# First attention of a fused transformer kernel: values of two steps on end in every second step, probabilities in eight buffers

## The reference

```python
# 32 query heads, 8 key/value heads, head size 16, after the rotation of q and k
scores = jnp.einsum('bhqd,bhkd->bhqk', q, k) / math.sqrt(HEAD_DIM)
scores = jnp.where(causal[None, None, :, :], scores, jnp.float32(-1e+20))
attn = jax.nn.softmax(scores, axis=-1)
out = jnp.einsum('bhqk,bhkd->bhqd', attn, v)
```

## Time and profile before

| | |
|---|---|
| median of the runs | 1273.1 us |
| the profiled execution, its own time | 1276.3 us |
| its span, from the first to the last instruction | 1274.6 us |
| busy: TensorE, weight loads, VectorE | 1179.1, 743.4, 928.0 us |
| busy: ScalarE, GpSimd | 655.5, 375.6 us |
| mean granted clock of TensorE | 0.94 |

### The profile page before, as it was taken

The page is one execution under the profiler, slowest core; times in us unless marked ns, Lnnn a source line. Parts: engine busy times, 40 slices in busy tenths (PEclk is TensorE's granted clock), DMA queues, the critical chain, the costliest instruction groups (busy, mean ns, idle before and its releaser), DMA issues.

```text
span 1274.6 us, 21543 instructions
## 1 busy us (share of the span) xinstructions
PE 1179.1 (93%) x6800; PEld 743.4 (58%) x6800; DVE 928.0 (73%) x2974; ACT 655.5 (51%) x1007; POOL 375.6 (29%) x505
## 2 busy tenths in 40 slices
PE   4998999999889998999989899999997999989888
PEld 1875343444358997545878644444432889855478
DVE  5789878999527878662768799899991578676365
ACT  1721556666555644444546026666666465445542
POOL 1431232222145520214624314111223455002261
PEclk9997679999899999899999958999999999989999
DMA  9465411121001013200250752112200100430001
GB/s 315 145 165 108 134 26 27 27 73 56 2 1 52 2 34 92 68 2 1 71 180 24 200 133 77 27 27 60 69 3 1 52 2 1 100 93 2 1 10 58
DMA packets 40309, 80.39 MB, mean 63 GB/s; under 512 B 6060, under 2 KB 7596, under 8 KB 40060
## 3 DMA queue, kind: packets, MB, share of 16 engines
q1 hardware_dynamic: 40200, 79.02, 21.8%
HBM read 48.98 MB, written 27.08 MB: 60 GB/s over the span
## 4 chain that ended last, share of the span: by engine, by line
PE 72%; DVE 14%; issue 5%; ACT 3%; DMA 3%; POOL 2%; SPq 1%; DVEq 0%; ACTq 0%; POOLq 0%
PE bank L1029 16%; PE bank L897 12%; PE bank L804 7%; PE bank L805 6%; PE bank L806 6%; DVE maxes L1247 5%; PE bank L1011 5%; DVE unused L1243 4%; PE bank L790 3%; PE bank L1005 3%; PE bank L907 2%; PE bank L829 2%; PE bank L831 2%; PE bank L830 2%; PE bank L879 1%
## 5 line engine op out<-in xcount | busy, mean ns | idle before, releaser
L1478 ACT ACTIVATE probs<-bank 128x1024 f32<-128x1024 f32 (+3 forms) x416 | 365.5, 911 | 308.1 <-PE bank L1011 225.6
L897 PE MATMUL bank<-ops 48*128 48x512 f32 (+3 forms) x960 | 318.0, 432 | 14.0 <-DVE maxes L1243 3.9
L1243 DVE CUSTOM_DVE_ANT_0 unused<-bank,causal 128x128 bf16<-128x128 f32 (+3 forms) x640 | 278.5, 485 | 46.5 <-PE bank L897 43.1
L1590 POOL TENSOR_SCALAR_AFFINE_SELECT probs<-probs 128x256 f32<-128x256 f32 (+1 forms) x256 | 118.9, 465 | 597.4 <-ACT probs L1478 596.4
L897 PEld LDWEIGHTS bank<-ops 48*128 48x128 f32 (+1 forms) x960 | 162.1, 204 | 194.8 <-DVE maxes L1243 81.3
L1029 PE MATMUL bank<-probs,v_mem 128*17 128x512 f32 (+6 forms) x1920 | 248.9, 526 | 2.1 <-ACT heads_raw L1465 1.5
L1247 DVE TENSOR_REDUCE maxes<-bank 128x1 f32<-128x512 f32 x320 | 206.8, 684 | 42.2 <-PE bank L897 41.4
L1011 PE MATMUL bank<-ops 50*128 50x512 f32 (+2 forms) x640 | 179.5, 455 | 4.4 <-ACT probs L1478 4.3
L1011 PEld LDWEIGHTS bank<-ops 50*128 50x128 f32 x640 | 88.8, 201 | 59.3 <-ACT probs L1478 30.5
L804 PE MATMUL bank<-ops,xT 128*128 128x512 f32 (+1 forms) x288 | 113.8, 395 | 5.7 <-DVE xT L1088 2.6
L1088 DVE TENSOR_TENSOR xT<-bank,xT 128x512 fp32r<-128x512 f32 (+1 forms) x96 | 61.5, 643 | 73.4 <-ACT xT L1357 73.2
(11 more groups left out here) (119 smaller groups left out, 1887.0 us busy)
## 6 DMA issues: line engine op xcount, KB each, us to landing
query_rows_dram<-ops SPq DMA_DIRECT2D x48, 256.0 KB, 3.8
ops<-query_rows_dram SPq DMA_DIRECT2D x64, 192.0 KB, 4.3
w_odd<-staging_wqkv SPq DMA_DIRECT2D x4, 1536.0 KB, 6.5
x<-x_dram SPq DMA_DIRECT2D x16, 256.0 KB, 5.6
ops<-features SPq DMA_DIRECT2D x64, 64.0 KB, 2.0
ops<-ops SPq DMA_DIRECT2D x16, 256.0 KB, 3.1
out_dram<-x SPq DMA_DIRECT2D x16, 256.0 KB, 2.0
staging_wqkv<-wqkv_dram SPq DMA_DIRECT2D x2, 1536.0 KB, 16.1
```

Of the source, the lines that this page charges most:

```text
L897: last = mm(dst[:, h * w:(h + 1) * w], queries(a, u)[rows, t // 4, hi, t % 4 * P:(t % 4 + 1) * P], keys(a, u, hi)[rows, HALF * kp:HALF * k ...
L1243: V.tensor_tensor_reduce(unused[:, masked % 3, 0:w], part, causal[:, HALF - w:], 1.0, NEG, ALU.add, ALU.max, dst).then_inc(s["max_done"].s ...
L1478: A.activation(probs[:, e % 6, :, 0:cols], scores[:, 2 * (e % 2):2 * (e % 2) + 2, 0:cols], ACT.Exp, scale=a.scale).then_inc(s["exp"].sem, 1)
L1590: G.affine_select(out=p, in_=p, compare_op=ALU.is_ge, fill=0.0, base=0, pattern=pattern, channel_multiplier=-1).then_inc(s["masked"].sem, 1)
```

## The change

The values of `A0` move from one per step to two in every second step, with the rule of `A1`: in a step `g` for which `g - lag` is odd, the values of `g - lag - 1` and `g - lag` are issued after one another. For `A0`, with a lag of two, these are the odd steps; for `A1`, with a lag of three, they are the even steps as before. `probs` grows from six buffers to eight, for both attentions, and the waits of the exponentials follow. Scores, ring items and their slots stay where they are.

```diff
+PROBS = 8
...
-        probs = sb("probs", [P, 6, 2, HALF])
+        probs = sb("probs", [P, PROBS, 2, HALF])
...
                         last = mm(heads[a.head_rows * h:a.head_rows * h + a.dim + 1, q0 - HALF * c:HALF],
-                                  v[:, j, a.kv_head(u, r, i), :], probs[:, e % 6, n, first:first + w],
+                                  v[:, j, a.kv_head(u, r, i), :], probs[:, e % PROBS, n, first:first + w],
...
                     ring_items(len(a.ring_at[g][1]))
-                    if a.row_tiles == 2:
-                        if a.lag <= g < a.units * ns + a.lag:
-                            value(g - a.lag)
-                    elif g % 2 == 0 and g > a.lag and g - a.lag < a.units * ns:
+                    if (g - a.lag) % 2 == 1 and g > a.lag and g - a.lag < a.units * ns:
                         value(g - a.lag - 1)
                         value(g - a.lag)
                     ring_items(len(a.ring_at[g][2]))
...
-                            if e >= 6:
-
-                                act.wait_ge(s["pv"].sem, s["pv"].at(b, a.step_of(e - 6) + 1))
-                            A.activation(probs[:, e % 6, :, 0:cols], scores[:, 2 * (e % 2):2 * (e % 2) + 2, 0:cols],
+                            if e >= PROBS:
+
+                                act.wait_ge(s["pv"].sem, s["pv"].at(b, a.step_of(e - PROBS) + 1))
+                            A.activation(probs[:, e % PROBS, :, 0:cols], scores[:, 2 * (e % 2):2 * (e % 2) + 2, 0:cols],
```

More of the change, by code:

```diff
@@ L1584, in attention @@
                         pool.wait_ge(s["exp"].sem, s["exp"].at(b, e + 1))
-                        p = probs[:, e % 6, :, 0:cols].rearrange("p n (i q) -> p n i q", q=w)[:, :, :, 0:P]
+                        p = probs[:, e % PROBS, :, 0:cols].rearrange("p n (i q) -> p n i q", q=w)[:, :, :, 0:P]
                         pattern = [[0, 2], [0, cols // w], [1, P]] if cols > w else [[0, 2], [1, P]]
                         if cols == w:
-                            p = probs[:, e % 6, :, 0:P]
+                            p = probs[:, e % PROBS, :, 0:P]
                         G.affine_select(out=p, in_=p, compare_op=ALU.is_ge, fill=0.0, base=0,
```

## The result

The changed kernel takes 1371.11 us (median of 4 runs, 1368.66 to 1373.26) against 1273.92 for the kernel before (four runs): a ratio of 1.076, 95% interval 1.073 to 1.080. It is slower, as forecast, but by 97 us where 17 were forecast, and far outside the range, which ended at 1306.

A forecast was written before the change was run, and what follows sets the result against it. VectorE's work plus its idle time was taken to bound full-clock units. Units +18.7, half-clock stretches -3.2 and tails +2.0 sum to +17.5 us on 1276.3, forecast as 1290 us against the 1273.1 median; range 1264 to 1306.

The forecast's parts named there:

- What bounds a full-clock unit: First attention: a unit lasts VectorE's work plus its idle time, 26.32 and 1.98 of 28.30 us.
- Second attention and eight buffers at 0: Second attention keeps its order, and the first attention's exponentials stay covered with eight buffers: no cost, no gain.
- A pair of 512 takes 1.84 us: Two 512-wide value blocks on end keep TensorE 1.84 us, against 0.98 for a single one.
- VectorE's dry times behind steps 7, 9 and 3: First attention: VectorE without work 1.17, 1.04 and 0.67 us behind these pairs, from 0.31, 0.18 and 0.66.
- Step 1: First attention, values 10 and 11: absence about 1.8 us against 1.57 of VectorE backlog, 0.2 us new dry time.
- step 11: First attention, values 8 and 9: 2.5 us of VectorE backlog against 2.65 of absence, 0.15 us new dry time.
- +1.56 us per unit: Net added VectorE idle time per full-clock unit of the first attention; over 12 units, +18.7 us.
- The tails, +1.0 each: End of each attention, blocks without ring maxima: ScalarE runs dry at two pairs, partly offset; +2.0 us in all.
- Half-clock stretches: Five stretches at granted clock 0.50, TensorE setting the pace: 8 switches removed, -3.2 us.
- two more stretches on top of the sum: Rival: the granted clock falls more often, each stretch costing 6.2 us, giving 1302 us; chance 0.11.
- TensorE sets the pace: Rival: removed tiling-mode switches count in full-clock units, giving about 1258 us; chance 0.17.
- it balances: Rival: even steps' dry times vanish and odd ones grow by less than 0.86 us, 1270 to 1276 us; chance 0.16.

The follow-up runs named there:

- equal filling: Each score of the first attention's even steps computed three times, in the changed kernel (1317.11 us) and in the kernel before (1300.31 us).
- the two wide pairs alone, with step 6 filled: Against the changed kernel, only values 4, 5 and 6, 7 paired in the first attention, and step 6's scores computed three times: 1308.80 us.
- filling in step 0: Against the changed kernel, only values 4, 5 and 6, 7 paired in the first attention, and step 0's scores computed three times: 1358.77 us.
- the kernel with narrow pairs: Against the kernel before, only the first attention's values of steps 2, 3 and 10, 11 (256 and 128 columns wide) paired: 1320.03 us.
- the kernel with the wide pairs: Against the kernel before, only the first attention's values 4, 5 and 6, 7 (512 wide) paired, in steps 7 and 9: 1308.15 us.

## Why the prediction was wrong

- *What bounds a full-clock unit*: right in the main. VectorE's work stays at 26.3 to 27.0 us. Of the 0.8 us that pairing adds with equal filling, 0.5 is VectorE's idle time (3.8 to 4.3 us).
- *Second attention and eight buffers at 0*: right, 0.999 for the buffers alone, and the second attention, from its first copy of `heads_raw` to its last, lasts the same within 0.4 us.
- *A pair of 512 takes 1.84 us, and VectorE's dry times behind steps 7, 9 and 3*: right to 0.01 us at full clock. Step 1 came as forecast too (0.22 for 0.2); step 11 was measured only behind filling.
- *+1.56 us per unit*: the right sign, size unsettled. With equal filling it is 0.8, though the 0.86 behind each of steps 7 and 9 came out; for the two wide pairs alone, with step 6 filled, 1.1 where the forecast had 0.86 + 0.86 less 0.32 to 0.5. The changed kernel itself has no unit without a half-clock stretch, so its own price at full clock was not measured.
- *The tails, +1.0 each*: in the second sequence, from the third-last copy of `heads_raw` to the last, at full clock and equally filled, it is 21.7 us with pairs and 21.0 without: +0.7.
- *The ring's part of the loss*: 160 of the 192 blocks have the ring, 13.3 units. At 0.8 to 1.56 us, with the tails, that is an estimated 12 to 23 us of the 97.
- *Half-clock stretches*: the step that failed. The forecast kept them as they were (-3.2 us) and put their increase among the rivals, "two more stretches on top of the sum", 1302 us, with a chance of 0.11. There are 32 more, 208 us more at half clock. The other 74 to 85 us, which are a remainder and not a measurement, fall to them: 0.36 to 0.41 us lost per us at half clock. The traces give a like price where units with and without a fall can be compared: 0.37 in the kernel before (the unit around 174.0 us lasts 35.9 us in place of 28.3, with 20.5 at half clock), 0.3 to 0.5 elsewhere. The forecast's own price, 6.2 us for a stretch of 20.4, is 0.30; what it missed is how much half-clock time there would be, 208 us where even the rival had some 41.
- *Why it was sized so low*: the argument against it was that the second attention, already in pairs, holds 1.00. In that stretch it does, after as before, but it does not carry over to the first. A likely reason, which no run tests, is that in the first attention VectorE fills 93% of a unit and TensorE waits for banks between pairs, while in the second VectorE has a third of its time free. The mechanism stood in the rival's own text, with the fall at 174.0 us as its sample, and was priced as two events instead of as something that comes back in each of 16 units. That the direction came out right owes little to the sum: its own part of the loss is a quarter or less.
- *TensorE sets the pace, it balances*: neither came. The kernel got slower, and no time saved by removed switches shows in it.
- Open: what decides that the clock falls. Shown is that emptying every second step of its value lowers it, that filling can restore it to 1.00 for most of the attention, and that where the filling stands matters by 50 us for the same amount. Not shown is a rule that foretells the place; falls recur at the same place in unit after unit and jump when a step's content moves.

## What to carry to other kernels

Where the granted clock of TensorE has already fallen once inside a steady loop, treat it as a term of every iteration, not as a disturbance: a reordering that leaves TensorE waiting for another engine for some steps can cost several times what the wait itself costs. Compute the other engine's dry time from its backlog and TensorE's absence; that worked to 0.01 us behind the two wide pairs. To tell the two apart on the chip, add harmless matmuls in the loop: if the kernel gets faster with more work, it was the clock. Try more than one place, and judge by the half-clock time in the trace: filling in step 0 made a kernel slower that filling in step 6 left as it was.

## What the runs showed of the hardware

- Redundant matmuls made the changed kernel 54 us faster (1371 to 1317, mean granted clock 0.868 to 0.955) and the kernel with narrow pairs 35 us faster (1320 to 1285, 0.896 to 0.957).
- In the kernel with the wide pairs, the same redundant matmuls moved from step 6 to step 0 made it 50 us slower (1309 to 1359).
- The falls keep step with the units: in the run with step 0 filled, four units in a row (copies of `heads_raw` at 203.39, 237.50, 271.61, 305.74 and 339.86 us) lasted 34.1 us each, with two half-clock stretches at the same places of each.
